# Graph network on one core: GpSimd's index copies are issued two gathers before their use, and the preparation runs in another order

## What is computed

```
def _gat_conv(x, src, dst, W, al, ar, b, act):
    z = (x @ W).reshape(N, H, F)                       # H = 4 heads, F = 64
    el = jnp.sum(z * al, axis=-1); er = jnp.sum(z * ar, axis=-1)
    e = jax.nn.leaky_relu(el[src] + er[dst], 0.2)
    ex = jnp.exp(e - segment_max(e, dst)[dst])
    alpha = ex / segment_sum(ex, dst)[dst]
    return act(segment_sum(z[src] * alpha[..., None], dst) + b)
```

## Time and profile before

| | |
|---|---|
| median of 3 runs | 7162.34 us (7157.12 to 7165.81) |
| profiled execution, its own time | 7210.36 us |
| its span | 7208.7 us |
| POOL busy, whole span | 3474.6 us (48%), 4137 instructions |
| DVE busy | 4171.6 us (58%) |
| PE busy | 4435.8 us (62%) |
| ACT busy | 2131.3 us (30%) |
| mean granted TensorE clock | 0.758 of full speed |

### The profile page before, as it was taken

The page is one execution under the profiler, slowest core; times in us unless marked ns, Lnnn a source line. Parts: engine busy times, 40 slices in busy tenths (PEclk is TensorE's granted clock), DMA queues, the critical chain, the costliest instruction groups (busy, mean ns, idle before and its releaser), DMA issues.

```text
span 7208.7 us, 120783 instructions
## 1 busy us (share of the span) xinstructions
PE 4435.8 (62%) x28861; PEld 2889.9 (40%) x28861; DVE 4171.6 (58%) x13512; ACT 2131.3 (30%) x5941; POOL 3474.6 (48%) x4137
## 2 busy tenths in 40 slices
PE   1566556666666674544544455545569888888875
PEld 1333333333333343222222222222257766676664
DVE  4777757777778764666666666666661111224444
ACT  0444434444455431333333333333310000000000
POOL 2777777777777714777777777777500000000000
PEclk9767766677677676666666666666689999999998
DMA  5455545555555532544444454444439989899977
GB/s 90 132 155 149 152 126 147 153 160 154 149 152 158 146 109 64 133 128 123 129 132 124 129 135 130 132 122 133 124 135 415 386 365 416 339 416 400 367 323 282
DMA packets 913170, 1390.70 MB, mean 193 GB/s; under 512 B 481527, under 2 KB 661905, under 8 KB 896598
## 3 DMA queue, kind: packets, MB, share of 16 engines
q1 hardware_dynamic: 576605, 879.74, 35.0%
q0 software_dynamic: 128976, 222.12, 13.7%
q10 hardware_dynamic: 207332, 286.15, 11.6%
HBM read 1014.17 MB, written 373.27 MB: 192 GB/s over the span
## 4 chain that ended last, share of the span: by engine, by line
issue 24%; DVE 21%; DMA 15%; PE 12%; POOL 11%; DVEq 7%; SPq 4%; ACT 3%; another core or an unknown queue 2%; ACTq 1%; POOLq 1%
POOL arena L818 9%; DMA arena<-adj_w_d 8%; DMA arena<-adj_c_d 4%; DVE arena L1038 4%; PE bank L1831 3%; PE bank L1832 3%; PE bank L1835 2%; DVEq L1052 2%; DVE arena L1061 2%; ACT arena L1966 2%; DVE arena L1039 1%; DVE arena L1173 1%; SPq L536 1%; DVE arena L1068 1%
## 5 line engine op out<-in xcount | busy, mean ns | idle before, releaser
L818 POOL DMA_INDIRECT arena<-table_d,arena x3136 | 3142.3, 1002 | 1346.7 <-issue 1112.0
L1681 PE MATMUL bank<-arena 128*128 128x500 f16 x3750 | 1352.2, 507 | 1479.3 <-issue 778.5
L1681 PEld LDWEIGHTS bank<-arena 128*128 128x128 f16 x3750 | 438.9, 125 | 2179.6 <-issue 1887.2
L1966 ACT ACTIVATE arena<-arena 128x128 f16<-128x128 f16 x3750 | 1126.2, 401 | 85.3 <-issue 58.9
L1702 PE MATMUL bank<-arena 128*65 128x40 f32 x7500 | 669.6, 253 | 533.7 <-issue 340.0
L1831 PE MATMUL bank<-arena 125*128 125x250 f16 x3750 | 859.4, 274 | 177.3 <-DMA arena<-adj_w_d 132.6
L1702 PEld LDWEIGHTS bank<-arena 128*65 128x65 f32 x7500 | 625.2, 167 | 663.5 <-issue 476.6
L1832 PE MATMUL bank<-arena 125*128 125x250 f16 x3750 | 855.4, 273 | 0.0
L1038 DVE TENSOR_SCALAR arena<-arena 128x500 f16<-128x500 f16 x1875 | 689.5, 368 | 192.9 <-issue 115.1
L2034 ACT ACTIVATE arena<-arena 128x600 f32<-128x600 f32 x250 | 176.4, 705 | 1954.2 <-DVEq L1175 1054.6
L1683 PE MATMUL bank<-arena 128*128 128x500 f16 x1875 | 687.9, 481 | 49.6 <-issue 48.3
(11 more groups left out here) (262 smaller groups left out, 4235.0 us busy)
## 6 DMA issues: line engine op xcount, KB each, us to landing
arena<-adj_w_d SPq DMA_DIRECT2D x720, 625.0 KB, 10.6
arena<-adj_c_d SPq DMA_DIRECT2D x345, 625.0 KB, 11.3
adj_w_d<-arena ACTq DMA_DIRECT2D x125, 1250.0 KB
arena<-msg_d SPq DMA_DIRECT2D x1250, 103.5 KB
msg_d<-arena POOLq DMA_DIRECT2D x196, 552.0 KB
adj_c_d<-arena ACTq DMA_DIRECT2D x125, 625.0 KB
arena<-table_d,arena POOLq DMA_INDIRECT x3136
arena<-in_edge_features ACTq DMA_DIRECT2D x625, 51.0 KB
```

What stands on the lines that cost most here:

```text
L818: g_.indirect_dma_start(ring[:, i, k * XC:(k + 1) * XC], None, table_d, bass.IndirectOffsetOnAxis(ap=idx_cur[:, i, k:k + 1], axis=0)).then ...
L1681: mm(wb, lhsT=row_oh[:, slot, c, i, :], rhs=col_oh[:, slot, c, :], start=(c == 0 and i == 0), stop=(c == CH - 1 and i == 1))
L1966: last = act_(row_oh[:, slot, c, i, :], row_oh[:, slot, c, 2, :], ACT.Copy, scale=rec[:, c * REC + 2 + i:c * REC + 3 + i])
```

## The change

It has two parts.

The first moves the copy of four indices. In `block`, gathers 2, 6, 10 and 14 of a block are each preceded by the copy for gathers 4, 8, 12 of the same block and 0 of the next. The wait on `idx_here` stays where it was, ahead of the first gather that uses the four. The first copy of a layer stands ahead of the wait for the table. The number of copies, waits and gathers stays.

The second reorders the preparation. VectorE makes `row_idx` as soon as `hi` is there and reports it, then does `table0_vector` and `starts_vector`, and then the rest of the records. TensorE does the 100 products first and the two tiny ones after. ScalarE instead of SP stores the table of layer 0. SP stores the starts first and then the records; it still reads the starts back after both. GpSimd waits for the indices instead of the records.

```diff
+AHEAD_IDX = 2
-("wgat_cleared", "v_made", "ptr_rows_wanted", "ew_max", "ew_top", "rec_made", "ptr_made", "items_made", "pace_made")
+("wgat_cleared", "v_made", "ptr_rows_wanted", "ew_max", "ew_top", "idx_made", "ptr_made", "rec_made", "items_made", "pace_made")
 # prep_sync
-            sp.wait_ge(s("prep_step"), PREP["rec_made"])
-            sp.dma_start(rec_d.rearrange(...), rec_all.rearrange(...)).then_inc(s("rec_stored"), 16)
             sp.wait_ge(s("prep_step"), PREP["ptr_made"])
             ...
             sp.dma_start(ptr_d[:, NW:NW + 1], ptr_end).then_inc(s("items_out"), 16)
+            sp.wait_ge(s("prep_step"), PREP["rec_made"])
+            sp.dma_start(rec_d.rearrange(...), rec_all.rearrange(...)).then_inc(s("rec_stored"), 16)
             sp.wait_ge(s("items_out"), 64)
             ...
-            sp.wait_ge(s("table_made"), 1)
-            sp.dma_start(table_rows(), xt).then_inc(s("table_stored"), 16)
 # blocks_pool
+            def copy_indices(j, i, k):
+                g_.tensor_copy(idx_cur[:, i, k:k + IDX], row_idx[:, bass.ds(j * BK + k, IDX)]).then_inc(s("idx_here"), 1)
 # block
+                    if k % IDX == IDX - AHEAD_IDX:
+                        following = k + AHEAD_IDX
+                        if following < BK:
+                            copy_indices(j, i, following)
+                        elif not last:
+                            copy_indices(j + 1, (i + 1) % RING, 0)
                     if k % IDX == 0:
-                        g_.tensor_copy(idx_cur[:, i, k:k + IDX], row_idx[:, bass.ds(j * BK + k, IDX)]).then_inc(s("idx_here"), 1)
                         wait_reg(pool, s("idx_here"), ...)
 ...
+            copy_indices(0, 0, 0)
             pool.wait_ge(s("table_stored"), 16 * (layer + 1))
 # gpsimd program
-            pool.wait_ge(s("prep_step"), PREP["rec_made"])
+            pool.wait_ge(s("prep_step"), PREP["idx_made"])
 # prep_vector, after hi is made
+            v.scalar_tensor_tensor(t0, hi, -float(NT), srcf, ALU.mult, ALU.add)
+            d.drain()
+            v.scalar_tensor_tensor(row_idx, t0, float(T), hi, ALU.mult, ALU.add)
+            d.drain().then_inc(s("prep_step"), 1)
+            table0_vector(d)
+            starts_vector(d)
 ...
             prep_vector(d)
-            starts_vector(d)
-            table0_vector(d)
 # prep_tensor: the two tiny products now stand after the 100 of the table
 # scalar program, in front of the store of er_d
+                if layer == 0:
+                    act.dma_start(table_rows(), xt).then_inc(s("table_stored"), 16)
```

More of the change, by code:

```diff
@@ L422, in first @@
             return isinstance(b, int) and b == 0
-        PREP = {name: i + 1 for i, name in enumerate(("wgat_cleared", "v_made", "ptr_rows_wanted", "ew_max", "ew_top", "rec_made", "ptr_made", "items_made", "pace_made"))}
+        PREP = {name: i + 1 for i, name in enumerate(("wgat_cleared", "v_made", "ptr_rows_wanted", "ew_max", "ew_top", "idx_made", "ptr_made", "rec_made", "items_made", "pace_made"))}
         def prep_sync(sp):
@@ L433, in prep_sync @@
             sp.dma_start(x_sb, nodes(a["x"])).then_inc(s("x_loaded"), 16)
-            sp.wait_ge(s("prep_step"), PREP["rec_made"])
-            sp.dma_start(rec_d.rearrange("(j p c) f -> p j (c f)", p=P, c=BK), rec_all.rearrange("p (j c) f -> p j (c f)", c=BK)).then_inc(s("rec_stored"), 16)
             sp.wait_ge(s("prep_step"), PREP["ptr_made"])
@@ L442, in prep_sync @@
             sp.dma_start(ptr_d[:, NW:NW + 1], ptr_end).then_inc(s("items_out"), 16)
+            sp.wait_ge(s("prep_step"), PREP["rec_made"])
+            sp.dma_start(rec_d.rearrange("(j p c) f -> p j (c f)", p=P, c=BK), rec_all.rearrange("p (j c) f -> p j (c f)", c=BK)).then_inc(s("rec_stored"), 16)
             sp.wait_ge(s("items_out"), 64)
@@ L805, in ready, with block @@
                 pool.sem_inc(s("msg_ready"), 1)
-            def block(j, i, uses, former):
+            def copy_indices(j, i, k):
+                g_.tensor_copy(idx_cur[:, i, k:k + IDX], row_idx[:, bass.ds(j * BK + k, IDX)]).then_inc(s("idx_here"), 1)
+            def block(j, i, uses, former, last=False):
                 if not isinstance(j, int) or j >= RING or layer:
@@ L837, in blocks_pool @@
             for i in range(NBLK % RING):
-                block(it * RING + i, i, it + uses_before[i], former_uses(it, i))
+                block(it * RING + i, i, it + uses_before[i], former_uses(it, i), last=i + 1 == NBLK % RING)
             last = NBLK - 1
@@ L896, in prep_vector @@
             v.tensor_scalar(part, ew, ews[:, 0:1], None, ALU.mult)
-            v.scalar_tensor_tensor(t0, hi, -float(NT), srcf, ALU.mult, ALU.add)
             d.drain()
@@ L903, in prep_vector @@
             v.scalar_tensor_tensor(srcf, hi, float(WN), srcf, ALU.mult, ALU.add)
-            v.scalar_tensor_tensor(row_idx, t0, float(T), hi, ALU.mult, ALU.add)
             d.drain()
@@ L1664, in prep_tensor @@
             pe.wait_ge(s("consts_made"), 1)
[L1665 to L1668, removed]
             pe.wait_ge(s("xT_loaded"), 16)
@@ L1673, in prep_tensor @@
             last.then_inc(s("el_psum"), 1)
+            pe.wait_ge(s("prep_step"), PREP["ew_max"])
+            mm(bank[6][0:1, 0:P], lhsT=ews[:, 3:4], rhs=ident, start=True, stop=True).then_inc(s("top_xt"), 1)
+            pe.wait_ge(s("prep_step"), PREP["ew_top"])
+            mm(bank[6][:, 256:257], lhsT=ones[0:1, :], rhs=ews[0:1, 2:3], start=True, stop=True).then_inc(s("top_xb"), 1)
         def seg_mms(out, ef_slot, w, oh):
```

## The result

| | before | after |
|---|---|---|
| median, beside each other | 7164.08 us (4 runs) | 6775.48 us (6769.08 to 6788.27, 4 runs) |
| ratio | | 0.9459, 95% interval 0.9442 to 0.9477 |
| span of the profiled execution | 7208.7 us | 6767.4 us |
| POOL busy | 3474.6 us (48%) | 3514.8 us (52%) |
| mean granted TensorE clock | 0.758 | 0.782 |

The kernel became 388.6 us faster. The direction and both places are right. The sizes of all three terms are not, and the term of the preparation has the wrong sign as well.

What follows compares the result with a forecast made beforehand. POOL was taken to bound layer 1, and the consumers' own pace layer 0. Preparation -9, layer 0 -61 and layer 1 -183 gave -253 us from 7162.3, forecast 6908 us, 80% range 6855 to 6980.

Steps and rivals of the forecast that it cites:

- the term of the preparation: Start to window loop: the reordered preparation lets the loop start earlier, -9 us (bounds -12 to +5).
- What bounds layer 1: Layer 1: GpSimd (POOL) sets the pace, as VectorE waited 557.7 us before its logits; gain -183 us.
- The cost of the wait behind a copy: GpSimd's gather after a copy: the wait costs 0.49 us, 392 times a layer, 192 us of POOL's time.
- My bound of 0.69: Upper bound of the saving per copy, in us: the copy vanishes beside its neighbours, 270 us a layer.
- Layer 0: Layer 0: VectorE goes at its own pace, 19.17 us a group; only message waits go, -61 us (-95 to -25).
- my slow case: Preparation: small stores as slow as before, records leave at 97 us, starts read at 121, 5 us later.
- the one that I leaned to: Preparation: small stores run freely, records leave at 80.5 us, reads of the starts come at 104, 12 us earlier.
- The head start: Preparation: POOL starts gathering at about 80 instead of 129.3 us, 50 us earlier, covering layer 0's first waits.
- the slower side: Convolutions: TensorE's clock falls after denser loops; at 0.80 it costs 362 us, total 7271 us; chance 0.03.
- The gap: Rival, GpSimd's 0.79 us idle behind a copy stays: layer 1 gains nothing, total 7092 us; chance 0.07.
- The chain of the three engines: Rival, layer 1: VectorE, ScalarE and TensorE become the bound at 18.5 us a group, total 6992 us; chance 0.10.
- my free copy: Rival: the copy costs GpSimd nothing, layer 1 gains 270 us at 17.1 us a group, total 6822 us; chance 0.05.

Runs made afterwards that it cites:

- the undisturbed execution: The kernel before, unchanged, profiled a second time: 7168.25 us, ratio 0.9998, span 7170.7 us.
- the last run above: One copy of 16 indices a block, two gathers ahead, with the preparation of the kernel before: 6699.77 us, ratio 0.9337 of the kernel before.

## Why the prediction was wrong
**What bounds layer 1**: right. GpSimd, by the waits of VectorE; it still does after (some 330 us of waits left, and GpSimd's own idle time in front of a gather is the usual 0.30 or 0.16 us, whatever ended it).

**The cost of the wait behind a copy**: the mechanism was right, the term mis-sized. I took the 0.30 us in front of any gather as fixed. Behind a copy it is 0.16, so 0.63 us are saved and not 0.49: 392 x 0.63 = 247 us. Measured were 236 from GpSimd's first gather to its last and 235 in the groups, where I had 183; the stores' longer waits for landed rows took most of the difference from 247. My bound of 0.69 held it, but the range that I built used 0.44 to 0.55 only. I had written the bounds down and then narrowed the range by taste.

**Layer 0**: this is the step that failed. "There VectorE is fed in time, and goes at a pace of its own ... 19.17 us each". It was fed in time because this one execution had thrown the consumers back; their undisturbed pace is 18.0 us, and in the undisturbed execution GpSimd's 19.3 us bound them. The 19.17 us were no pace at all: groups 40 to 56, right behind the worst stretch, took 20.4 us each and groups 56 to 120 took 18.9, with TensorE late now and then in both, and the mean came out beside GpSimd's rate by luck. From first to last group layer 0 went from 2395.0 us (second profile of before) to 2227.0, 168 us or 1.35 a group, less 8 us because the first group comes later: 160 us (last group at 2571.9 and 2411.9 us), where I had 61. The profile held two warnings that I read past: two engines with the same rate to 1%, and an execution 48 us over the median. I carried the 48 us over whole and took paces from the layer in which they lay: the last group of layer 0 is 38 us later in the first profile than in the second, as much as the two spans differ by. Counted from the undisturbed profile: up to the end of layer 0 -160, layer 1 -225, the gap between them -6, the untouched end -13, together the 403 us between the spans 7170.7 and 6767.4.

**The preparation**: forecast -9, measured +6.3, beyond the bound of +5. TensorE's turn came as worked out (tiny product at 48.64 us, VectorE waiting 6.25 us, indices at 60.3, first gather at 79.62). Three sizes behind it were off. The small stores didn't run freely: with no records ahead of them SP still issued them for 25.2 us where it had been 30.8, so the records had been little of what held them up, and the records left at 92.2 us, nearer the 97 of my slow case than the 80.5 of the one that I leaned to. The records landed in 35.1 us and not in 21.6, and the starts came back at 130.6 instead of 104 to 121. In all profiles with the new preparation, in which gathers run beside the records, they took 27.5 to 35.5 us, in all others 21.6; that the gathers are the reason isn't shown by itself. The third helped: from the starts to the loop it took 38.7 us and not 46.5. The head start, which I had as one of two reasons for layer 0's gain, adds nothing to the other that these runs can tell: the copies alone feed the layer (13 us of message waits left), the head start alone doesn't (148 us left).

**The rivals**: the convolutions kept their clock of 0.96, so the slower side has nothing for it. The gap did not stay. The chain of the three engines did become a bound, in layer 0 at 18.0 us and not in layer 1, where 17.4 us a group is still GpSimd's: with one copy a block it went down to 16.9, under the 17.1 of my free copy. The free copy, 0.05 with 6822 us, was nearest in the copy's price.

## What to carry to other kernels
A wait right behind a small instruction on an engine that runs without a break costs the whole hand-over of what comes next (0.6 us here, 784 times); one gather between the two was enough to hide it, and fewer, larger copies (16 indices for the 0.20 us of 4) did as much without any reordering. Try the smaller edit first: here it was one line, and the reordered preparation brought nothing that the runs can tell beside it. An engine whose busy share is 72% can be the bound of a stage: look at whether its idle time is ended by others or by itself. If the profiled execution is 48 us above the median, find where the 48 us lie before any pace is taken from it, and profile the kernel twice. A wait that is named "remote" or "issue" in one profile and has a name in the next is a sign of missing events; go by starts then.

## What the runs showed of the hardware that I had not expected
A gather issued by GpSimd starts 0.16 us after a copy that it doesn't wait for and 0.30 us after a gather or a plain store. A copy of 128x16 indices takes 0.20 to 0.21 us, one of 128x4 0.19 to 0.20. With one copy a block in place (`IDX = 16` in the kernel before) the consumers of layer 0 went at 17.7 us a group from group 24 on, with the copies ahead at 17.9 to 18.0. The old preparation isn't the reason, for the last run above has it too and went at 17.9; each number is from a single profile, and the cause stays open.
